# Regrouping FFN units, block transposes and one scatter wait in the batch schedule of a two-layer kernel

## The reference

```python
# layer 1, per sequence
out = x + (ln(x; g1,b1) @ (sf_w*mask).T + sf_b)
q, k, v = ln(out; g2,b2) @ (wq, wk, wv).T + biases       # 16 heads of 16
att = relu(q k^T / 4) * causal;  att /= att.sum(-1) + 1e-9
out = out + (att v) @ wo.T + bo
out = out + relu(ln(out; g3,b3) @ ff1.T + b) @ ff2.T + b  # 256 -> 1024 -> 256
x = ln(x + out)                                           # called ln4 in the kernel
# layer 2: each token goes to the expert with the largest x . centroid (8 experts)
y = expert FFN of that expert (256 -> 1024 -> 256), gated by sigmoid of the affinity
x = ln(x + y)
```

## Time and profile before

| | us |
|---|---|
| median of 3 runs | 845.33 (844.70 to 845.36) |
| the profiled execution | 845.33 |
| its span, first to last instruction | 843.6 |
| TensorE busy | 819.3 (97%) |
| VectorE busy | 527.0 (62%) |
| ScalarE busy | 347.7 (41%) |
| GpSimd busy | 281.3 (33%) |

### The profile page before, as it was taken

One profiled execution on the slowest core, in us unless ns is written; L12 is line 12 of the kernel. 1 busy time (PEld: TensorE's weight loads), 2 busy tenths in 40 slices (PEclk: granted clock), 3 DMA queues, 4 the chain that ended last, 5 costly groups with the idle time before them and its releaser, 6 DMA issues.

```text
span 843.6 us, 19374 instructions
## 1 busy us (share of the span) xinstructions
PE 819.3 (97%) x7250; PEld 547.0 (65%) x7250; DVE 527.0 (62%) x1526; ACT 347.7 (41%) x579; POOL 281.3 (33%) x392
## 2 busy tenths in 40 slices
PE   8999999999999999999999999999999999999994
PEld 5545476476466557548547646869989967776673
DVE  5475368757757856866787755524678555565652
ACT  1443414523532541641541442333333466577670
POOL 3503111421503413223143151325455454434422
PEclk9999999999999999999999999999999999999998
DMA  6710300220030020040030042334643897978930
GB/s 251 213 51 26 77 2 1 62 66 1 27 101 0 27 52 1 1 126 2 1 101 2 2 129 100 112 88 134 217 165 134 305 329 254 330 296 293 342 135 16
DMA packets 63939, 96.44 MB, mean 114 GB/s; under 512 B 39332, under 2 KB 52261, under 8 KB 55911
## 3 DMA queue, kind: packets, MB, share of 16 engines
q1 hardware_dynamic: 58550, 83.56, 29.7%
q0 software_dynamic: 4864, 11.10, 4.3%
q10 hardware_dynamic: 432, 0.54, 0.2%
HBM read 84.22 MB, written 11.23 MB: 113 GB/s over the span
## 4 chain that ended last, share of the span: by engine, by line
PE 71%; DVE 17%; ACT 5%; issue 5%; POOL 1%; DMA 1%; another core or an unknown queue 0%; DVEq 0%; ACTq 0%; POOLq 0%
PE ps L638 11%; PE ps L740 10%; PE ps L758 9%; PE ps L632 7%; PE ps L571 6%; PE ps L595 6%; PE ps L804 4%; PE ps L780 4%; DVE w_sb L1112 3%; PE ps L603 3%; PE ps L465 3%; DVE x3x L1112 3%; ACT arena L1620 2%; DVE st_ln L929 2%; DVE arena L1042 2%
## 5 line engine op out<-in xcount | busy, mean ns | idle before, releaser
L638 PE MATMUL ps<-ff2T,hT 128*128 128x256 f32 x512 | 121.6, 385 | 0.2 <-ACT hT L1612 0.2
L632 PE MATMUL ps<-x3x,ff1T 128*128 128x512 f32 x256 | 118.2, 605 | 0.1
L1620 ACT ACTIVATE arena<-ps 128x1536 f32<-128x1536 f32 (+3 forms) x49 | 65.1, 1328 | 113.2 <-DVE arena L1042 113.2
L638 PEld LDWEIGHTS ps<-ff2T,hT 128*128 128x128 f32 x512 | 94.3, 190 | 21.0 <-issue 8.1
L758 PE MATMUL ps<-w_sb,arena 128*128 x400 | 95.6, 382 | 0.0
L1836 POOL TENSOR_TENSOR rs_ln<-mv_ln,eps 128x4 f32<-128x4 f32 x24 | 5.2, 216 | 265.9 <-DVE mv_ln L936 265.9
L632 PEld LDWEIGHTS ps<-x3x,ff1T 128*128 128x128 f32 x256 | 46.0, 189 | 60.3 <-issue 53.0
L758 PEld LDWEIGHTS ps<-w_sb,arena 128*128 128x128 f32 x400 | 72.2, 190 | 16.0 <-issue 8.2
L571 PE MATMUL ps<-arena 32*128 32x512 f32 (+7 forms) x896 | 73.0, 434 | 2.1 <-ACT hT L1061 1.4
L1042 DVE SCALAR_TENSOR_TENSOR arena<-ps,arena 128x512 f32<-128x512 f32 (+4 forms) x59 | 45.0, 770 | 47.4 <-PE ps L595 27.8
L595 PE MATMUL ps<-arena 64*32 64x256 f32 (+7 forms) x1584 | 56.9, 399 | 0.7 <-issue 0.7
(11 more groups left out here) (239 smaller groups left out, 1567.1 us busy)
## 6 DMA issues: line engine op xcount, KB each, us to landing
arena<-in_w SPq DMA_DIRECT2D x27, 1024.0 KB
hT<-in_w SPq DMA_DIRECT2D x16, 1024.0 KB
wts<-in_w SPq DMA_DIRECT2D x9, 1024.0 KB
w_sb<-in_w SPq DMA_DIRECT2D x8, 1024.0 KB, 6.4
token_store<-x SPq DMA_DIRECT2D x8, 520.0 KB, 3.9
arena<-in_x SPq DMA_DIRECT2D x8, 512.0 KB, 4.0
w_sb<-in_x SPq DMA_DIRECT2D x48, 64.0 KB, 2.5
arena<-in_epack SPq DMA_DIRECT2D x18, 134.0 KB
```

The lines of the kernel that those rows point to most:

```text
L632: last = eng.matmul(ps[:, 6 + m % 2, :], ff1T[:, kd, m * P:(m + 1) * P], xT3[:, kd, :], start=kd == 0, stop=kd == KD - 1)
L638: last = eng.matmul(quarter(6, t), hT[:, m, t * P:(t + 1) * P], ff2T[:, m, :], start=m == 0, stop=m == FM - 1)
L1620: eng.activation(o, i, ACT.Relu).then_inc(s_sa, 1)
```

## The change

It does six things.
- `UNITS` and `UNITS1`: FFN2 units are now four matmuls (`pe_ffn2`), two to a token tile. For b of 2 and more FFN1 unit 7 moves from step 5 to step 6, tile 0 is split over steps 6 and 7, and tile 1 stays in step 8. For b = 1 all of tile 0 stands in step 6 and none in step 7.
- The rank matmuls use bank 7 in place of 6, and the wait for the rank's result moves from the first FFN2 unit to FFN1 unit 7.
- `TURN3`: the transposes of LN3 rows stand 8 before step 0 and 8 in step 0 (before: 8, 6 and 2). `TURN4`: 11 in step 3 and 5 in step 4 (before: 4, 9 and 3 in steps 2, 3 and 4).
- `act_gain3` does half 0 in step 0 and half 1 in step 1, not both in step 1.
- `act_ln4` follows the eviction of FFN1 unit 0 and no longer precedes it.
- GpSimd's scatter waits for the eighth of the ten weighings of the batch, not for the last.

```diff
--- before.py
+++ after.py
@@ -95,18 +95,15 @@
 BUFFERS0, BUFFERS = (0, 1, 2, 3, 0, 1, 2, 3, 0), (0, 1, 2, 0, 1, 2, 0, 1, 0)
 
 
-
-UNITS = ((), (), (0, 1), (2,), (3, 4), (5, 6, 7), (8, 9, 10), (11,), (12, 13, 14, 15))
-
-UNITS1 = ((), (0, 1), (2, 3), (4,), (5, 6), (7,)) + UNITS[6:]
+UNITS = ((), (), (0, 1), (2,), (3, 4), (5, 6), (7, 8), (9,), (10, 11))
+
+UNITS1 = ((), (0, 1), (2, 3), (4,), (5, 6), (7,), (8, 9), (), (10, 11))
 
 VALUES = (range(2), range(2, NKT))
 
 
-
 N_TURN = 16
-TURN3 = (range(8), range(8, 14), range(14, N_TURN))
-TURN4 = (range(4), range(4, 13), range(13, N_TURN))
+TURN3, TURN4 = 8, 11
 
 W2_LOADS = ((0,), (1,), (2,), (3,), (4,), (), (7,), (5, 6))
 N_ARENA = 16320
@@ -623,9 +620,9 @@
             if m < 2 and b:
 
                 eng.wait_ge(s_r3, 2 * b - 1 + m)
-            if 0 < b < NB - 1 and m == 5:
-
-                eng.wait_ge(s_afd, b)
+            if 0 < b < NB - 1 and m in (5, 7):
+
+                eng.wait_ge(s_afd if m == 5 else s_rkd, b)
             if m >= 2:
                 eng.wait_ge(s_f1e, FM * b + m - 1)
             for kd in range(KD):
@@ -640,23 +637,17 @@
             if t % 2 and FM - 1 in part:
                 last.then_inc(s_f2, 1)
 
+        def pe_ffn2(eng, b, t, half):
+            if t == 0 and half == 0:
+                eng.wait_ge(s_f1e, FM * b + FM)
+            pe_ffn2_part(eng, b, t, range(4 * half, 4 * half + 4))
+
         def pe_unit(eng, f, k):
 
             if k < FM:
                 pe_ffn1(eng, f, k)
-                return
-            if k == FM:
-                eng.wait_ge(s_f1e, FM * f + FM)
-                if 0 < f < NB - 1:
-
-                    eng.wait_ge(s_rkd, f)
-            t, q = (k - FM) // 4, (k - FM) % 4
-            pe_ffn2_part(eng, f, t, (2 * q, 2 * q + 1))
-
-        def pe_units(eng, f, t, half):
-
-            for q in (2 * half, 2 * half + 1):
-                pe_unit(eng, f, FM + 4 * t + q)
+            else:
+                pe_ffn2(eng, f, (k - FM) // 2, k % 2)
 
         def pe_ln4_T(eng, g):
             eng.wait_ge(s_xh["ln4"], g + 1)
@@ -703,7 +694,7 @@
             eng.wait_ge(s_oh, g + 1)
             if g < NB - 2:
 
-                eng.wait_ge(s_f1e, FM * (g + 1) + 7)
+                eng.wait_ge(s_f1e, FM * (g + 1) + 6)
 
             def sums(t):
                 return ps[:, bank, P + t * NE:P + (NT + 1) * NE]
@@ -833,7 +824,7 @@
                     pe_ahead(eng, n)
                     continue
                 if b > 1 and n == 0:
-                    pe_units(eng, g, NT - 1, 1)
+                    pe_ffn2(eng, g, NT - 1, 1)
                 if b > 1 and n < len(VALUES):
                     pe_values(eng, b, 4, VALUES[n])
                 for k in (UNITS1 if b == 1 else UNITS)[n]:
@@ -841,7 +832,7 @@
                 if n == 4 and g >= 0:
                     pe_affinity(eng, g, 7)
                 if n == 5 and g >= 0:
-                    pe_rank(eng, g, 6)
+                    pe_rank(eng, g, 7)
             for w in (AVS - 2, AVS - 1):
                 pe_weigh(eng, b, w)
             if b == 0:
@@ -850,19 +841,19 @@
                 pe_proj_o(eng, b)
             elif more:
                 pe_sf(eng, b + 1)
-                pe_units(eng, f, NT - 2, 0)
+                pe_ffn2(eng, f, NT - 2, 0)
                 pe_proj_o(eng, b)
-                pe_units(eng, f, NT - 2, 1)
+                pe_ffn2(eng, f, NT - 2, 1)
                 pe_ln2_T(eng, b + 1)
-                pe_units(eng, f, NT - 1, 0)
+                pe_ffn2(eng, f, NT - 1, 0)
             else:
-                pe_units(eng, f, NT - 2, 0)
-                pe_units(eng, f, NT - 2, 1)
+                pe_ffn2(eng, f, NT - 2, 0)
+                pe_ffn2(eng, f, NT - 2, 1)
 
                 eng.wait_ge(s_r3, 2 * f + 1)
                 slot_pe_x_T(eng, 0)
-                pe_units(eng, f, NT - 1, 0)
-                pe_units(eng, f, NT - 1, 1)
+                pe_ffn2(eng, f, NT - 1, 0)
+                pe_ffn2(eng, f, NT - 1, 1)
 
                 eng.wait_ge(s_sa, STEPS * NB)
                 slot_pe_layer1(eng, 0, range(3))
@@ -885,12 +876,12 @@
             slot_pe_layer1(eng, 1, range(FM - 2))
             pe_ln3_T(eng, f)
             slot_pe_layer1(eng, 1, range(FM - 2, FM))
-            for k in range(FM + 4 * NT):
+            for k in range(2 * FM):
                 if k == 4:
                     pe_ln4_T(eng, f - 1)
                 if k == FM:
                     pe_affinity(eng, f - 1)
-                if k == FM + 6:
+                if k == FM + 3:
                     pe_rank(eng, f - 1)
                 pe_unit(eng, f, k)
             eng.wait_ge(s_tab, 1)
@@ -1429,22 +1420,23 @@
             if b == 0:
                 dve_values(eng, b)
             if b > 1:
-                dve_turn_rows3(eng, f, TURN3[0])
+                dve_turn_rows3(eng, f, range(TURN3))
             for n in range(STEPS):
                 if n == 6 and g >= 0:
-                    dve_rank(eng, g, 6)
+                    dve_rank(eng, g, 7)
                 if b == 0:
                     dve_first_scores(eng, n)
                 else:
                     dve_scores(eng, b, n)
                 if b > 1 and n == 0:
-                    dve_turn_rows3(eng, f, TURN3[1])
+                    dve_turn_rows3(eng, f, range(TURN3, N_TURN))
                 if b > 1 and n == 1:
-                    dve_turn_rows3(eng, f, TURN3[2])
                     dve_mean_var(eng, "ln4", dve_add_ffn(eng, g, 1))
                     dve_values(eng, b, 4)
-                if g >= 0 and 2 <= n < 5:
-                    dve_turn_rows4(eng, g, TURN4[n - 2])
+                if g >= 0 and n == 3:
+                    dve_turn_rows4(eng, g, range(TURN4))
+                if g >= 0 and n == 4:
+                    dve_turn_rows4(eng, g, range(TURN4, N_TURN))
                 if b and more and n == 4:
                     dve_turn_input(eng, b + 1)
                 if b == 0 and n in (1, 2):
@@ -1765,15 +1757,14 @@
                     act_queries(eng, 1, (1,), (6, 6))
                     act_keys(eng, 1, (1,), (7, 5))
                     act_ln3_T(eng, f)
-                if b > 1 and n == 1:
-                    for kd in range(KD):
-                        act_gain3(eng, f, kd)
-                if n == 2 and g >= 0:
-                    act_ln4(eng, g)
+                if b > 1 and n < KD:
+                    act_gain3(eng, f, n)
                 if b:
                     for k in (UNITS1 if b == 1 else UNITS)[n]:
                         if k < FM:
                             act_ffn1(eng, f, k)
+                        if k == 0 and g >= 0:
+                            act_ln4(eng, g)
             if more and b:
                 act_ln2_T(eng, b + 1)
 
@@ -1959,7 +1950,7 @@
                 slot_pool_rstd(eng, 1, 0)
             if g >= 0:
 
-                eng.wait_ge(s_av, AVS * (b + 1))
+                eng.wait_ge(s_av, AVS * b + AVS - 2)
                 pool_scatter_ids(eng, g)
             if more:
                 pool_rstd_ln2(eng, b + 1)
```

## The result

The changed kernel takes 860.5 us (median of 4 runs, 860.25 to 860.82) against 845.3 (4 runs, 844.70 to 845.36): ratio 1.0181, 95% interval [1.0164, 1.0199]. It is slower, by 15.2 us where 10.4 were forecast: outside the forecast's own 852.5 to 859, and at the far end of the range. The profiled execution took 860.26 for a span of 858.5. It is 14.9 longer than the one before, and all of it is in the first layer: the start of FFN1 that follows batch 7 goes from 544.88 to 560.24.

A forecast was written before the change was run, and what follows sets the result against it. TensorE, 97% busy, was taken as the bound, so late instruction starts count. 6 x (1.50 + 0.14) = 9.8 plus 0.6 for batch 1 gives 10.4 on 845.33: 855.7 us; own range 852.5 to 859, full range 850.5 to 860.5.

The forecast's parts named there:

- Scatter: GpSimd's four indirect DMAs, issued after the eighth weighing instead of the tenth: no gain and no cost, 0 us.
- steps 5 to 8: In batches 2 to 7, FFN2 waits for FFN1 unit 7's eviction behind relu 6: 1.50 us a batch, bounds 0 and 2.14.
- the stall of batch 7: Step 5 weighing takes 3.49 us against 1.46 in batch 5; 2.0 us lost, kept unchanged, 2 us either way in range.
- the second layer: Layer after the changed batches: starts later by the sum, with no fixed time seen that would absorb it.
- steps 0 to 4: Moved transposes and gains delay scores 2 by 0.26 and affinity by 0.14: 0.14 us a batch, bounds -0.81 and +0.90.
- Step 6: TensorE stands ahead of the first FFN2 matmul until ScalarE evicts FFN1 unit 7 after relu 6: 1.50 us a batch.
- Batch 1: Step 6 gets 16 instructions, step 7 none, so scores 8 wait for relu 7: 0.62 us late.
- 0.90 in steps 0 to 4: Rival: two transposes ahead of mask 1 and the gain ahead of relu 1 not absorbed, six batches: 860.3 us, 13%.
- hidden wait: Rival: the FFN2 wait in step 6 is hidden, leaving 6 x 0.14 + 0.6 = 1.4 us: 846.8 us, 7%.
- faster: Rival: the 0.81 us idle ahead of affinity goes in six batches and step 6 costs nothing: 841.0 us, 5%.
- mask 4 earlier: Condition for the faster rival: mask 4 at 360.6, so the last five transposes are done by 363.6 (forecast 364.4).

The follow-up runs named there:

- the run with late gathers: Kernel before, with GpSimd's first four layer-2 gathers in batch 7 waiting for the fifth weighing: 843.23 us, ratio 0.9978.
- the 4, 7 and 5 split: Kernel before, with the 16 LN4 transposes split 4, 7, 5 over steps 2, 3 and 4 (before 4, 9, 3): 840.73 us, ratio 0.9947.

## Why the prediction was right and where it failed
- **The step that failed** is "Scatter": "an earlier one brings 0. It costs 0 too". It measured 5.06 us over five batches, and undoing it alone gives 5.4 back. The argument had looked at GpSimd's own queue and at what the scatter might do to VectorE's mask. Those held: no wait of another engine for GpSimd grew. It hadn't asked what TensorE does while GpSimd issues, although the trace of before had the case in the earlier trace rows. With the scatter undone the kernel takes 855.05, against 855.7 forecast for the rest. That this is so close is in part luck: in the ledger steps 5 to 8, the stall of batch 7 and the second layer came out 1.4 us lower, steps 0 to 4 and the start-up 0.8 us higher. The forecast also took the eighth weighing for the moment of the issues, which LN1's rstd sets.
- **The stall of batch 7** was seen and priced, and left without a cause. GpSimd's timeline, which I hadn't put beside the other two engines, shows the four gathers; the run with late gathers removes it. So it wasn't something that shifts by chance, and the change made its like in five batches by moving four issues onto a weighing. The Trainium skill ("Runtime: NRT & Kernel Launch", Instruction fetch mechanics) has a sequencer fetch its code ahead, mostly hidden. That rule kept the stall where it was, and it was right that code alone doesn't place it: it goes with the gathers. In the trace of before the instruction queue has no packet between 502 and 504 (the nearest are at 495.25 and 512.25). Whether the gathers disturb that fetching is only argued. It would fit TensorE, which stops in its densest stretch, but VectorE stops with it, and around the stall of batch 5 in the changed kernel (396.28 to 399.15) the instruction queue has no packet from 392 to 404.
- **Step 6, right, slightly over-sized.** 1.50 forecast, 1.28 in most batches. Scores 6 were put at 371.21 and start at 380.18, 8.97 later, which is the drift of the batches before; measured from there unit 7 starts where it was put (372.34 and 8.97 is 381.31). The mask came 0.11 earlier than reckoned, and the eviction 1.35 after relu 6 started, not 1.45: ScalarE overlaps the two. In batches 3 and 7 VectorE reaches mask 6 later (1.52 and 1.82 after scores 6 start, 1.32 in batch 5), and the loss is 1.48 and 1.77.
- **Steps 0 to 4, right.** Scores 2 are 0.23 late (0.26 forecast), the idle ahead of affinity goes from 0.81 to 0.76 and is now ended by the block transposes. Net 0.18 for 0.14. For that idle the forecast's own times give 0.69 (0.81 + 0.14 - 0.26), where it says 0.6 in one place and 0.5 in another.
- **Batch 1, right.** Scores 8 now show 0.74 us of wait for relu 7; the batch is 0.61 longer for 0.62.
- **The range** had 860.5 as its end for a reason that did not occur (0.90 in steps 0 to 4). The total came near it through a cost that had no term and no bound of its own: the scatter's bounds were 0 and 0.
- The rivals "hidden wait" and "faster" are refuted for this change. But the condition named for the second (mask 4 earlier) is what the 4, 7 and 5 split meets, and it brings 4.5 of the 4.9 us named for it.

## What to carry to other kernels
Before an issue of indirect DMAs is moved, lay its whole stretch (here 4.8 us for four) over TensorE's timeline, and keep it off stretches of many short instructions; FFN1's long matmuls carried it free here. Look for its place in the trace, since the wait that the program names may not be the one that ends last. A stall that ends by "issue" or by nothing in the program is a lead: look at what every other engine does in the microseconds ahead of it before it is set down as noise. And keep the eviction that a matmul needs from standing behind longer work in the same queue: moving the unit one step earlier brought 0.8 of 1.28 us; putting the eviction ahead of the relu wasn't run.

## What the runs showed of the hardware
- Four indirect DMAs issued by GpSimd, 0.96 to 1.03 us each and 4.8 us together, stop TensorE in a weighing (64 loads and 64 short matmuls, 1.89 us undisturbed) in every case where they ended more than 1 us inside it. It goes on about 0.75 us after the last issue ends, in batch 3 of the changed kernel (256.83, 257.58), in the kernel before with the early scatter (254.50, 255.25), and 0.78 after it in batch 7 (503.27, 504.05). VectorE stops in the same stretch in batch 7 and goes on at the same moment. The cause below that isn't settled.
- Eight plain DMAs issued back to back by GpSimd, 0.55 us each, do not do this to the weighing. The Trainium skill ("GPSIMD Engine Reference", When to use GPSIMD) says that the descriptors of any DMA issued there are generated by a pair of GpSimd's cores; by that alone both kinds would be alike, and the weighing shows that they aren't.
- Extra plain DMAs from GpSimd ahead of the scatter do bring idle times of 2.3 to 5.6 us on VectorE that nothing in the program ends, in two batches of five, and at times stops of TensorE (1.73 us, until 466.46) and of GpSimd (until 464.52); that is 7 us in both kernels that had them in this form. Some come after the scatter's issues, one ahead of them. From SyncE four such DMAs bring idle times of 1.5 to 2.0 us on VectorE in three batches, which cost 0.8 us in all. What picks the batch, and whether this and the stop in the weighing have one cause, no run here tells.
